# Quantised cross-attention and expert layer: first query among the keys, values quantised by chunk and transposed by DMA

## Chip, cores and metric

The kernel runs on one core of a Trainium2 chip. The metric is the device time of one execution in microseconds (us). The kernel is written engine by engine: TensorE (PE), VectorE (DVE), ScalarE (ACT), GpSimd (POOL) and SyncE (SP, which only issues DMAs) each have an instruction stream of their own and meet at semaphores.

## What is computed

2048 tokens (`x`, 4 x 512 rows) and 2048 context rows, both of width 512. One layer of cross-attention with 16 heads of 32 columns, then a mixture of 32 experts (4 for each token) and a shared expert. Only the attention, and of it only its preparation, is touched here:

```python
q = (layernorm(x) @ Wq + bq) / sqrt(32)        # 2048 x 512, 16 heads of 32
k, v = split(ctx @ Wkv + bkv)                  # 2048 x 512 each
q = fq_sym(q, axis=-1)                         # 8-bit, a scale for each row and head
k = fq_sym(k, axis=-1)                         # likewise
v = fq_sym(v, axis=rows)                       # 8-bit, ONE scale for each column, over all 2048 rows
p = fq_unsigned(softmax(q @ k.T))              # 8-bit probabilities, 2048 x 2048 for each head
x = x + (p @ v) @ Wp + bp
x = x + experts(layernorm(x))
```

The scale of a column of `v` needs that column's largest value over all 2048 context rows, so no value can be rounded before the last context row has been projected.

## The kernel before

**Keys phase.** `keys(g)` runs for g = 0 to 3, each time over four tiles of 128 context rows (i = 4g + r). PE transposes a context tile into the bank `psT` (L1579), ACT copies it out (L1457), PE projects keys (L1589, L1592). DVE rounds them (L1504 to L1512: largest value, scale, reciprocal, 8-bit, back to f32) and, with ACT (L1477, L1479), splits them into three bf16 parts; SP transposes the parts into `kT` by DMA (L1377, a 128 x 2048 bf16 transpose). DVE also takes the statistics of one tile of `x` (L539) and POOL normalises it (L587 to L609); SP stores it to `xn_dram` (L1357). At the end of each g, PE projects the values, turned, in four chunks m of 128 columns (L1608, 8 matmul passes each), ACT adds the bias and writes `vT[:, m, ...]` (L1469, semaphore `v_ev`), and DVE takes the largest value of each chunk (L1525 for g = 0, L1528 later).

**The bridge.** After g = 3, in this order. PE makes the first query tile: `pe_query(pe, 0, ...)`, four transposes (L385), ACT's copy (L1484), a bias matmul (L395) and eight passes (L396) into `psP`. DVE joins the maxima of the values (L1532), makes scale and reciprocal (L1551, L1553), rounds the four chunks to 8 bits, `vT8` (L1558, 128 x 2048 each), and only then rounds the query tile (L545, L551, L555). POOL widens chunks 0 and 1 to bf16, `vTb` (L1433), ACT chunks 2 and 3 (L1487). PE then transposes `vTb` in 16 blocks (L1629) into the banks `psT` and `psO`, which ACT (L1490) and DVE (L1563) copy in turn into `v`. POOL spreads the query tile (L622) and multiplies the four chunks of `Wp` by the values' scales (L1439); SP transposes the query tile by DMA into `qT[0]` (L1390). All engines wait for the last block of `v` before they enter the attention.

**Attention.** `pairs(eng, step)` runs 256 units (16 query tiles x 16 heads), written out by hand for each engine. In unit n PE makes scores of 128 queries x 2048 keys in two halves (L446) into `psS[0]` and `psS[1]`; DVE copies each half to `S` with its running maximum (L565, L581); POOL makes the bias (L638); ACT does the exponential to 8 bits, `p8` (L526); SP transposes `p8` by DMA into `pT` (L708); POOL widens to `pb` (L649), three units behind; PE multiplies by `v` (L461), LAG = 7 units behind. `S`, `p8`, `pT` and `pb` have four slots each, so unit n waits for unit n - 4. In between, in the same streams, the next query tile is made (heads 2 to 10) and earlier tiles are finished. Of the memory used by the keys phase, most is used again by the attention.

**Experts.** They follow when all units are done, from about 840 us on, and aren't touched.

Of the kernel before, what the change touches and what calls it, by code (L numbers as in the profile page):

```python
# [21 lines left out]
def attention_and_experts(nc, x, ctx_in, wq, wkv, wp, biases, bv, router, ebias, moe_w, out):  # L22
# [33 lines left out]
    with ExitStack() as es:  # L56
# [8 lines left out]
        psO = psAV[1]  # L65
# [65 lines left out]
        vT8 = cut(DC * TK // 4, I8).rearrange("p (c t) -> p c t", c=DC)  # L131
        k8 = cut(D // 4, I8)
        ks = [cut(D) for _ in range(2)]
# [3 lines left out]
        wkv_start = at[0]  # L137
# [3 lines left out]
        at[0] = phase_start  # L141
        S = [cut(TK) for _ in range(NS)]
        p8 = [cut(TK // 4, U8) for _ in range(NS)]
        pT = [cut(TK // 4, U16) for _ in range(NS)]
        pb = [cut(TK // 2, BF16).rearrange("p (j b q) -> p j b q", b=2, q=P) for _ in range(NS)]
# [4 lines left out]
        assert at[0] >= wkv_start  # L150
        qT = [cut(H * P // 2, BF16).rearrange("p (h q) -> p h q", h=H) for _ in range(2)]
        xn2T = cut(D).rearrange("p (c t) -> p c t", c=DC)

# [73 lines left out]
        v_cp_dve = sem("v_cp_dve")  # L227
# [53 lines left out]
        v_cp = sem("v_cp")  # L281
# [4 lines left out]
        v_tr = sem("v_tr")  # L286
        v_whole = sem("v_whole")
        v_whole_act = sem("v_whole_act")
# [83 lines left out]

        def pe_query(pe, t, stage):
# [13 lines left out]
            else:  # L387
                c = stage - 1
                if c == 0:
                    pe.wait_ge(query_ev, t + 1)  # L390
                    if due(t):
                        pe.wait_ge(q8_ready, t)
                    if due(t - 3):
                        pe.wait_ge(logits_cp, t - 3)
                    nc.tensor.matmul(psP[:], ones3[:], bias3[:, 0:D], start=True, stop=False)  # L395
                last = nc.tensor.matmul(psP[:], xnT[:, c, :], wq_sb[:, c, :], start=False, stop=(c == DC - 1))  # L396
# [41 lines left out]
        def pe_step(pe, tt, l):  # L438
# [102 lines left out]
        def dve_scale(dve, t):  # L541
# [3 lines left out]
            nc.vector.tensor_reduce(amax, hv(psP[:]), AX.X, ALU.max, apply_absolute_value=True).then_inc(q_amax, 1)  # L545

        def dve_whole(dve, t, p):
# [7 lines left out]
            nc.vector.scalar_tensor_tensor(hv(q8), hv(psP[:]), QSCALE, bc(rc, HD), ALU.mult, ALU.mult).then_inc(q8_ready, 1)  # L555
# [69 lines left out]
        def pool_step(pool, tt, l):  # L625
            n, p, h = PAIR * tt + l, l // H, l % H
            t = 2 * tt + p
            if there(t):
# [6 lines left out]
                if due(n - NS + 1):  # L635
# [3 lines left out]
                                            nsq[p][:, h:h + 1], LN255, ALU.mult, ALU.add).then_inc(bias_ready, 1)  # L639
            if not isinstance(n, int) or 0 <= n - BEHIND < TT * H:  # L640
# [36 lines left out]
        def sp_step(sp, tt, l):  # L677
# [32 lines left out]
            if h == 15 and there(t - 1):  # L710
# [3 lines left out]
                sp.dma_start(rows(out, t - 1), x1).then_inc(x1_stored, 16)  # L714

# [609 lines left out]
        def _(sp):  # L1325
# [65 lines left out]
            for b in range(2):  # L1391
                sp.wait_ge(keys_moved[b], 16 * KT // 2)
            sp.wait_ge(v_cp, KT // 2)
            sp.wait_ge(v_cp_dve, KT // 2)
# [9 lines left out]
        def _(pool):  # L1404
# [16 lines left out]
            for r in range(4):  # L1421
                normal(r, r)
            with pool.Fori(1, GK) as g:
# [3 lines left out]
            for m in range(DC // 2):  # L1427
                pool.wait_ge(v8_ready, m + 1)
                apart(pool, m + 1)
                if m == 0:  # L1430
                    pool.wait_ge(v_mm, 4 * GK)
                    pool.wait_ge(k_mm, KT)
# [253 lines left out]
```

## Time and profile before

| what | us |
|---|---|
| three runs | 1496.22, 1499.61, 1509.61 |
| median | 1499.61 |
| profiled execution, its own time | 1504.55 |
| span in the trace of that execution | 1502.6 |
| keys phase: start to the last value chunk out of PE | 0 to 149.8 |
| bridge: from there to the first score copy on DVE | 149.8 to 174.3 |
| attention units | 174.3 to about 841 |

The profile is one execution. Times in its views are microseconds from the start of the span. A row of the timeline gives start, duration, engine, line, operation, tiles, count, and in brackets how long the engine had been idle and what ended that. "SPq" rows are the time SP took to issue a DMA, not the transfer. The chain of waits is the chain of work that ended last, followed back step by step. The row of a stretch gives each engine's busy time in it, the clock that was granted to TensorE (1.00 is full speed) and the busy share of the 16 DMA engines.

### The profile page before, as it was taken

The page shows a single profiled execution, that of the slowest core. Times are in us where ns is not written, and L with a number is a line of the kernel's source. Part 1 is how long each engine was busy: PE and PEld are TensorE (multiplying, and loading weights), DVE is VectorE, ACT ScalarE, POOL GpSimd, SP SyncE. Part 2 cuts the span into 40 slices and gives each one's busy share as a digit, 9 for nine tenths or more (in the row PEclk, how much of TensorE's full clock was granted, in tenths as well). Part 3 has the DMA queues.
Part 4 walks back from the last instruction along what each step waited for, and adds up shares of the span by engine and source line. Part 5 has one row for each costly group of instructions (what it writes and reads, how often), then busy time and mean ns, then how long its engine had stood idle before and what let it go on. Part 6 is the DMA issues. An engine that isn't in the chain of part 4 may idle for free.

```text
span 1502.6 us, 28760 instructions
## 1 busy us (share of the span) xinstructions
PE 1300.7 (87%) x7954; PEld 647.3 (43%) x7955; DVE 989.5 (66%) x1847; ACT 794.2 (53%) x1022; POOL 871.5 (58%) x883
## 2 busy tenths in 40 slices
PE   7999678887888888888887588799999899999998
PEld 3333234443444444444444344344444444444443
DVE  7555699999999999999999257433333233323333
ACT  2222499998999999999999431122222121212221
POOL 3111388889899999999999403434343443444441
PEclk9999699999999999999999689999999999999999
DMA  9664178776676776676777365465666666665432
GB/s 267 159 157 98 32 130 142 135 141 133 140 146 142 141 144 133 139 141 139 145 137 131 103 247 183 158 180 112 190 186 188 190 151 162 158 179 123 83 57 72
DMA packets 387509, 217.60 MB, mean 145 GB/s; under 512 B 348279, under 2 KB 348407, under 8 KB 383234
## 3 DMA queue, kind: packets, MB, share of 16 engines
q1 hardware_dynamic: 369586, 182.34, 50.0%
q0 software_dynamic: 17872, 34.64, 12.5%
q8 instruction: 25, 0.41, 0.1%
q14 instruction: 26, 0.21, 0.1%
HBM read 104.47 MB, written 37.49 MB: 94 GB/s over the span
## 4 chain that ended last, share of the span: by engine, by line
PE 29%; issue 21%; DMA 17%; DVE 14%; POOL 10%; ACT 5%; SPq 2%; DVEq 2%; POOLq 1%; ACTq 0%
PE psS L773 14%; DMA out_y<-mem 11%; POOL mem L649 6%; DVE mem L565 4%; DVE mem L581 4%; PE psS L781 4%; DMA mem<-mem 3%; ACT mem L526 2%; PE psS L1608 2%; PE psS L446 2%; DMA mem<-xn_dram,mem 2%; POOL mem L638 1%; DVEq L1192 1%; PE psP L765 1%; PE psP L1589 1%
## 5 line engine op out<-in xcount | busy, mean ns | idle before, releaser
L526 ACT ACTIVATE mem<-mem 128x2048 uint8<-128x2048 f32 x256 | 535.3, 2093 | 46.0 <-POOL mem L638 41.2
L649 POOL TENSOR_SCALAR mem<-mem 128x2048 bf16<-128x2048 uint8 x256 | 486.2, 1899 | 28.3 <-DMA mem<-mem 9.2
L446 PE MATMUL psS<-mem 128*128 128x512 bf16 x1024 | 312.6, 388 | 97.8 <-DVE mem L565 49.1
L773 PE MATMUL psS<-mem 128*128 (+1 forms) x752 | 356.9, 617 | 0.1
L581 DVE TENSOR_SCALAR_CACHE_REDUCE mem<-psS,mem 128x1024 f32<-128x1024 f32 x256 | 328.1, 1282 | 0.9 <-PE psS L446 0.9
L565 DVE TENSOR_SCALAR_CACHE_REDUCE mem<-psS 128x1024 f32<-128x1024 f32 x256 | 313.0, 1223 | 15.0 <-PE psS L446 11.4
L807 DVE TENSOR_SCALAR mem<-psS 128x512 f32<-128x512 f32 x94 | 65.2, 693 | 344.3 <-PE psS L773 341.3
L1170 POOL DMA_INDIRECT out_y<-mem x78 | 124.0, 1589 | 189.3 <-DMA out_y<-mem 153.0
L801 ACT ACTIVATE mem<-mem 128x256 f32<-128x256 f32 x94 | 39.4, 419 | 360.8 <-DVE mem L807 360.8
L773 PEld LDWEIGHTS psS<-mem 128*128 128x128 f32 x752 | 139.9, 196 | 151.7 <-issue 148.8
L781 PE MATMUL psS<-mem 128*128 (+1 forms) x376 | 177.1, 592 | 1.0 <-ACT mem L795 1.0
L461 PEld LDWEIGHTS psAV<-mem 128*128 128x128 bf16 x4096 | 137.4, 96 | 86.9 <-POOL mem L649 36.7
L446 PEld LDWEIGHTS psS<-mem 128*128 128x128 bf16 x1024 | 67.9, 98 | 238.2 <-DVE mem L565 153.5
L1148 POOL DMA_INDIRECT mem<-xn_dram,mem x83 | 86.6, 1043 | 130.6 <-DVE mem L1281 91.1
L461 PE MATMUL psAV<-mem 128*128 128x32 bf16 x4096 | 142.7, 177 | 19.4 <-POOL mem L649 19.3
L789 ACT ACTIVATE mem<-psT 128x512 f32<-128x512 f32 x91 | 54.6, 600 | 123.7 <-PE psT L1201 90.7
L781 PEld LDWEIGHTS psS<-mem 128*128 128x128 f32 x376 | 70.9, 189 | 91.1 <-issue 89.7
L638 POOL TENSOR_SCALAR mem<-mem 128x1 f32<-128x1 f32 x256 | 68.0, 266 | 47.1 <-DVE mem L581 22.7
L1608 PE MATMUL psS<-mem 128*128 128x512 f32 x128 | 58.8, 613 | 9.5 <-ACT mem L1469 9.5
L396 PE MATMUL psP<-mem 128*128 128x512 f32 x128 | 66.5, 605 | 0.0
L1201 PEld LDWEIGHTS psT<-ident,mem 128*128 128x128 f32 x316 | 39.1, 142 | 63.4 <-issue 56.1
L417 PE MATMUL psAV<-mem 128*128 128x512 f32 x128 | 66.2, 602 | 0.0
(213 smaller groups left out, 1192.8 us busy)
## 6 DMA issues: line engine op xcount, KB each, us to landing
mem<-in_moe_w SPq DMA_DIRECT2D x33, 1536.0 KB, 8.1
xn_dram<-mem SPq DMA_DIRECT2D x33, 256.0 KB, 2.4
mem<-in_x SPq DMA_DIRECT2D x32, 256.0 KB, 3.1
mem<-xn_dram SPq DMA_DIRECT2D x32, 256.0 KB, 3.0
out_y<-mem SPq DMA_DIRECT2D x32, 256.0 KB, 2.3
mem<-mem SPq DMA_TRANSPOSE x288, 3.1
mem<-in_ctx_in SPq DMA_DIRECT2D x16, 256.0 KB, 3.2
mem<-out_y SPq DMA_DIRECT2D x16, 256.0 KB, 4.1
```

Of the source, the lines that this page charges most:

```text
L446: last = nc.tensor.matmul(psS[c][:, k * D:(k + 1) * D], qT[pm][:, hm, :], kT[:, hm, c * HALF + k * D:c * HALF + (k + 1) * D], start=True, ...
L461: last = nc.tensor.matmul(bank[:, ho * HD:(ho + 1) * HD], pb[slot][:, b // 2, b % 2, :], v[:, b, ho * HD:(ho + 1) * HD], start=(b == 0), s ...
L526: nc.scalar.activation(p8[slot], S[slot], ACT.Exp, bias=NB[:, slot:slot + 1], scale=sq[p][:, h:h + 1], accum_out=Z[p][:, h:h + 1]).then_in ...
L565: nc.vector.tensor_scalar(S[slot][:, 0:HALF], psS[0][:], 1.0, None, ALU.mult, ALU.max, accum_out=M[:, 2 * slot:2 * slot + 1]).then_inc(hal ...
L581: nc.vector.tensor_scalar(S[before][:, HALF:TK], psS[1][:], 1.0, M[:, 2 * before:2 * before + 1], ALU.mult, ALU.max, accum_out=M[:, 2 * be ...
L638: nc.gpsimd.tensor_scalar(NB[:, slot:slot + 1], M[:, 2 * slot + 1:2 * slot + 2], nsq[p][:, h:h + 1], LN255, ALU.mult, ALU.add).then_inc(bi ...
L649: nc.gpsimd.tensor_scalar(pb[slot], pT[slot].bitcast(U8).rearrange("p (j q b) -> p j b q", b=2, q=P), 1.0, 0.0, ALU.mult, ALU.add).then_in ...
L773: last = nc.tensor.matmul(bankG[o], xT[o if xo is None else xo][:, c, :], w(c * 2 * I, 2 * I), start=(c == 0), stop=(c == DC - 1))
L781: last = nc.tensor.matmul(bankY[o], hT[o][:, c, :], w(DC * 2 * I + c * D, D), start=(c == 0), stop=(c == I // P - 1))
L1148: nc.gpsimd.indirect_dma_start(out=xg[l], out_offset=None, in_=xn2_dram, in_offset=bass.IndirectOffsetOnAxis(list_column, 0), bounds_check ...
L1170: nc.gpsimd.indirect_dma_start(out=out, out_offset=bass.IndirectOffsetOnAxis(tile_rows[l][:, 0:1], 0), in_=y[l], in_offset=None, compute_o ...
L1608: last = nc.tensor.matmul(psS[m % 2][:, 0:D], wkv_sb[:, c, D + m * P:D + (m + 1) * P], cT[:, c, :], start=(c == 0), stop=(c == DC - 1))
```

## The change

1. The first query tile is made between `keys(0)` and `keys(1)`, on PE, ACT, DVE and POOL. It goes into `psS[1][:, D:2D]` in place of `psP`. Its DMA transpose into `qT[0]` (now in the memory of `ks`) is issued by SP after the last key transpose, ahead of the last store of normalised `x`.
2. On DVE the last group, `keys(3)`, is written out, and each value chunk is handled at once by `values(m)`: maximum, join, scale, reciprocal, rounding; then the next chunk.
3. POOL widens chunks 0 and 2, ACT chunks 1 and 3, with even and odd context rows put apart. SP transposes each by DMA straight into `v` (semaphore `v_moved`). PE's 16 blocks of transposes and the copies by ACT and DVE are gone.
4. No engine waits for `v` before the attention. PE waits for `v_moved` and `wp_scaled` in unit 7, POOL for `v_moved` ahead of the first `pb`. POOL scales `Wp` in units 0 and 1, two chunks in each. `pb` and `S` come first in the reused memory (`pb` lies over `vTb`), and `p8`, `pT`, `xn2T`, `qT[1]` lie behind `qT[0]`.

```diff
+        qT0 = mem[:, at[0]:at[0] + H * P // 2].bitcast(BF16).rearrange("p (h q) -> p h q", h=H)
+        ks = [cut(D) for _ in range(2)]
+        behind_keys = at[0]
...
+        def query_bank(t):
+            return psS[1][:, D:2 * D] if isinstance(t, int) and t == 0 else psP[:]
...
@@ pe_step @@
+                if isinstance(n, int) and n == LAG:
+                    pe.wait_ge(v_moved, 16 * DC)
+                    pe.wait_ge(wp_scaled, DC)
@@ pool_step, behind the bias of unit n, and ahead of pb @@
+                if isinstance(n, int) and n < DC // 2:
+                    for c in (2 * n, 2 * n + 1):
+                        nc.gpsimd.tensor_scalar(wp_sb[:, c, :], wp_sb[:, c, :], sv[:, c:c + 1], 1.0, ALU.mult,
+                                                    ALU.mult).then_inc(wp_scaled, 1)
...
+                if isinstance(m, int) and m == 0:
+                    pool.wait_ge(v_moved, 16 * DC)
@@ SP @@
             keys(GK - 1, False)
+            sp.wait_ge(q_spread, 1)
+            sp.dma_start_transpose(qT[0], qst.rearrange("p h j d -> p (h j d)")).then_inc(queries_moved[0], 16)
             store_normal(TT - 1, 3)
+            sp.wait_ge(query_tr, 1)
             sp.wait_ge(xn_stored, 16 * TT)
-            sp.wait_ge(query_tr, 1)
             sp.dma_start(xn, rows(xn_dram, 1)).then_inc(xn_in, 16)
-            sp.wait_ge(q_spread, 1)
-            sp.wait_ge(v_mm, 4 * GK)
-            sp.wait_ge(k_mm, KT)
-            sp.dma_start_transpose(qT[0], qst.rearrange("p h j d -> p (h j d)")).then_inc(queries_moved[0], 16)
...
+            for m in range(DC):
+                sp.wait_ge((v_whole, v_whole_act)[m % 2], m // 2 + 1)
+                sp.dma_start_transpose(v[:, :, m * P:(m + 1) * P], vTb[:, m, :]).then_inc(v_moved, 16)
             pairs(sp, sp_step)
@@ POOL @@
             for r in range(4):
                 normal(r, r)
+            pool.wait_ge(spread_zero, 1)
+            pool_scale(pool, 0, 0)
+            pool_spread(pool, 0)
...
+            for m in range(0, DC, 2):
                 pool.wait_ge(v8_ready, m + 1)
+                if m == 2:
                     pool.wait_ge(v_mm, 4 * GK)
+                nc.gpsimd.tensor_scalar(by_parity(vTb[:, m, :]), keyed(vT8[:, m, :]),
+                                            1.0, 0.0, ALU.mult, ALU.add).then_inc(v_whole, 1)
@@ ACT @@
             keys(0)
+            act.wait_ge(query_tr, 1)
+            nc.scalar.activation(xnT.rearrange("p c t -> p (c t)"), psT[:], ACT.Copy).then_inc(query_ev, 1)
             with act.Fori(1, GK) as g:
                 keys(g)
...
+            for m in range(1, DC, 2):
                 act.wait_ge(v8_ready, m + 1)
+                nc.scalar.activation(by_parity(vTb[:, m, :]), keyed(vT8[:, m, :]), ACT.Copy).then_inc(v_whole_act, 1)
@@ DVE, in keys(g) and behind it @@
+                    if last:
+                        values(m)
...
+            def values(m):
+                col = slice(m, m + 1)
+                dve.wait_ge(v_amax, KT + m - DC + 1)
+                nc.vector.tensor_tensor(svm[:, col], svm[:, col], vmax[:, col], ALU.max).then_inc(v_top, 1)
+                dve.wait_ge(v_top, GK - 2 + m + 1)
+                nc.vector.tensor_scalar(sv[:, col], svm[:, col], 1.0 / 127.0, 1e-8, ALU.mult, ALU.max).then_inc(v_scale, 1)
+                dve.wait_ge(v_scale, m + 1)
+                nc.vector.reciprocal(rv[:, col], sv[:, col]).then_inc(v_recip, 1)
+                dve.wait_ge(v_recip, m + 1)
+                if m == DC - 1:
+                    dve.wait_ge(xn_stored, 16 * TT)
+                nc.vector.tensor_scalar(vT8[:, m, :], vT[:, m, :], rv[:, col], None, ALU.mult).then_inc(v8_ready, 1)
...
             keys(0)
-            with dve.Fori(1, GK) as g:
-                keys(g)
+            dve_scale(dve, 0)
+            dve_whole(dve, 0, 0)
+            with dve.Fori(1, GK - 1) as g:
+                keys(g)
+            keys(GK - 1)
             pairs(dve, dve_step)
@@ PE @@
             keys(0)
+            pe.wait_ge(c_ev, 4)
             pe_query(pe, 0, 0)
             pe.wait_ge(w_q, 16)
             pe.wait_ge(bias_moved, 96)
             for stage in range(1, DC + 1):
                 pe_query(pe, 0, stage)
-            for b in range(KT):
-                if b >= 2:
-                    pe.wait_ge((v_cp, v_cp_dve)[b % 2], b // 2)
-                for m in range(DC):
...
+            with pe.Fori(1, GK) as g:
+                keys(g)
+            pe.wait_ge(c_ev, KT)
+            pe.wait_ge(k_whole, KT)
+            pe.wait_ge(v_ev, 4 * GK)
             for b in range(2):
                 pe.wait_ge(keys_moved[b], 16 * KT // 2)
             pairs(pe, pe_step)
```

## Rows read from the trace of the kernel before

**Rows 1.** The page: busy time, share of the span, instructions of each engine.

```profile
PE 1300.7 (87%) x7954; PEld 647.3 (43%) x7955; DVE 989.5 (66%) x1847; ACT 794.2 (53%) x1022; POOL 871.5 (58%) x883
```

**Rows 2.** Stretches: length, PE, PEld, DVE, ACT, POOL busy, clock, DMA share, GB/s.

```profile
150.00:187.50 37.50, 23.65 (x106) 11.28 (x105) 25.78 (x38) 16.06 (x18) 11.73 (x14) 0.68 0.15 31
225.00:300.00 75.00, 63.00 (x656) 33.12 (x655) 73.81 (x127) 68.63 (x72) 65.00 (x68) 1.00 0.81 139
```

**Rows 3.** The page, costliest groups: busy, mean ns, idle before and its releaser.

```profile
L649 POOL TENSOR_SCALAR mem<-mem 128x2048 bf16<-128x2048 uint8 x256 | 486.2, 1899 | 28.3 <-DMA mem<-mem 9.2
...
L581 DVE TENSOR_SCALAR_CACHE_REDUCE mem<-psS,mem 128x1024 f32<-128x1024 f32 x256 | 328.1, 1282 | 0.9 <-PE psS L446 0.9
L565 DVE TENSOR_SCALAR_CACHE_REDUCE mem<-psS 128x1024 f32<-128x1024 f32 x256 | 313.0, 1223 | 15.0 <-PE psS L446 11.4
```

**Rows 4.** Chain of waits across two group ends: start, us, what.

```profile
36.05 7.15 PE psS L1608 x16
...
48.89 0.70 DVE mem L1504
...
84.30 0.70 DVE mem L1504
```

**Rows 5.** Timeline: the first query tile on PE, and its load for it.

```profile
39.11 0.58 SPq L1379 DMA_DIRECT2D mem<-xn_dram  x1
...
149.65 0.60 PE L385 MATMUL psT<-ident,mem 128*128 128x128 f32 x4
...
151.56 3.70 PE L396 MATMUL psP<-mem 128*128 128x512 f32 x8
```

**Rows 6.** The line L1379 (that load): issue to landing.

```profile
DMA to landing us min/median/max: 3.0/3.0/3.0
```

**Rows 7.** Timeline of the last value chunks and the bridge.

```profile
142.78 1.28 DVE L1528 TENSOR_REDUCE mem<-mem 128x1 f32 x2
...
144.62 1.20 SPq L1357 DMA_DIRECT2D xn_dram<-mem  x1
...
146.50 0.69 ACT L1469 ACTIVATE mem<-psS,mem 128x512 f32 x1 [3.30 <-PE psS L1608]
...
149.94 0.69 ACT L1469 ACTIVATE mem<-psS,mem 128x512 f32 x1 [2.74 <-PE psS L1608]
...
150.76 0.69 DVE L1528 TENSOR_REDUCE mem<-mem 128x1 f32 x1 [2.75 <-ACT mem L1469]
...
152.28 8.15 DVE L1558 TENSOR_SCALAR mem<-mem 128x2048 int8<-128x2048 f32 x4
...
153.66 5.69 POOL L1433 TENSOR_SCALAR mem<-mem 128x2048 bf16<-128x2048 int8 x2 [9.61 <-DVE mem L1558]
...
160.46 1.91 ACT L1487 ACTIVATE mem<-mem 128x2048 bf16<-128x2048 int8 x1 [0.92 <-DVE mem L1558]
...
174.30 1.23 DVE L565 TENSOR_SCALAR_CACHE_REDUCE mem<-psS 128x1024 f32<-128x1024 f32 x1 [1.26 <-PE psS L446]
```

**Rows 8.** The line L1558: one instruction, min/median/max ns.

```profile
L1558 DVE TENSOR_SCALAR mem<-mem x4: 1279/2096/2920, 152.3 to 157.5; 128x2048 int8<-128x2048 f32 x4
```

**Rows 9.** Timeline of the first units, and the query transpose before them.

```profile
164.06 1.92 SPq L1390 DMA_TRANSPOSE mem<-mem  x1
...
179.30 0.27 POOL L638 TENSOR_SCALAR mem<-mem 128x1 f32<-128x1 f32 x1 [12.58 <-DVE mem L581]
...
183.94 5.32 SPq L708 DMA_TRANSPOSE mem<-mem  x3
...
187.17 1.90 POOL L649 TENSOR_SCALAR mem<-mem 128x2048 bf16<-128x2048 uint8 x1
```

**Rows 10.** The line L1390 (query transpose): issue to landing.

```profile
DMA to landing us min/median/max: 6.0/6.0/6.0
```

**Rows 11.** Stretches of the first units (columns as in group 2).

```profile
173.00:182.00 9.00, 6.77 (x17) 2.26 (x18) 6.20 (x12) 0.83 (x2) 0.54 (x2) 0.50 0.00 0
182.00:185.00 3.00, 1.87 (x7) 0.26 (x5) 3.00 (x5) 3.00 (x3) 0.27 (x1) 0.92 0.00 0
```

More of the change, by code:

```diff
@@ L141, in attention_and_experts @@
         at[0] = phase_start
+        pb = [cut(TK // 2, BF16).rearrange("p (j b q) -> p j b q", b=2, q=P) for _ in range(NS)]
         S = [cut(TK) for _ in range(NS)]
-        p8 = [cut(TK // 4, U8) for _ in range(NS)]
-        pT = [cut(TK // 4, U16) for _ in range(NS)]
-        pb = [cut(TK // 2, BF16).rearrange("p (j b q) -> p j b q", b=2, q=P) for _ in range(NS)]
         an = cut(D)
@@ L149, in attention_and_experts @@
         xn2 = cut(D)
-        assert at[0] >= wkv_start
-        qT = [cut(H * P // 2, BF16).rearrange("p (h q) -> p h q", h=H) for _ in range(2)]
+        at[0] = behind_keys
+        p8 = [cut(TK // 4, U8) for _ in range(NS)]
+        pT = [cut(TK // 4, U16) for _ in range(NS)]
         xn2T = cut(D).rearrange("p (c t) -> p c t", c=DC)
+        qT = [qT0, cut(H * P // 2, BF16).rearrange("p (h q) -> p h q", h=H)]
         at[0] = 0
@@ L280, in attention_and_experts @@
         v_top = sem("v_top")
-        v_cp = sem("v_cp")
         v_ev = sem("v_ev")
@@ L285, in attention_and_experts @@
         v_scale = sem("v_scale")
-        v_tr = sem("v_tr")
         v_whole = sem("v_whole")
+        v_moved = sem("v_moved")
         v_whole_act = sem("v_whole_act")
@@ L394, in pe_query @@
                         pe.wait_ge(logits_cp, t - 3)
[L395 to L396 removed]
+                    nc.tensor.matmul(query_bank(t), ones3[:], bias3[:, 0:D], start=True, stop=False)
+                last = nc.tensor.matmul(query_bank(t), xnT[:, c, :], wq_sb[:, c, :], start=False, stop=(c == DC - 1))
                 if c == DC - 1:
@@ L1520, in keys @@
                 for m in range(DC):
+                    last = isinstance(g, int) and g == GK - 1
+                    first = isinstance(g, int) and g == 0
                     dve.wait_ge(v_ev, 4 * g + m + 1)
-                    src = vT[:, m, bass.ds(g * D, D)] if not isinstance(g, int) else vT[:, m, g * D:(g + 1) * D]
-                    if isinstance(g, int):
-                        nc.vector.tensor_reduce(svm[:, m:m + 1], src, AX.X, ALU.max, apply_absolute_value=True).then_inc(
-                            v_amax, 1)
-                    else:
-                        nc.vector.tensor_reduce(vmax[:, m:m + 1], src, AX.X, ALU.max, apply_absolute_value=True).then_inc(
-                            v_amax, 1)
@@ L1530, in keys @@
-                dve.wait_ge(v_amax, 4 * g + DC)
-                if not isinstance(g, int):
-                    nc.vector.tensor_tensor(svm, svm, vmax, ALU.max).then_inc(v_top, 1)
-                    dve.wait_ge(v_top, g)
+                    part = vT[:, m, bass.ds(g * D, D)] if not isinstance(g, int) else vT[:, m, g * D:(g + 1) * D]
+                    nc.vector.tensor_reduce((svm if first else vmax)[:, m:m + 1], part, AX.X, ALU.max,
+                                                apply_absolute_value=True).then_inc(v_amax, 1)
@@ new lines, in keys @@
+                    if last:
+                        values(m)
+                if not last:
+                    dve.wait_ge(v_amax, 4 * g + DC)
+                    if not first:
+                        nc.vector.tensor_tensor(svm, svm, vmax, ALU.max).then_inc(v_top, 1)
+                        dve.wait_ge(v_top, g)
+            def values(m):
[10 more added lines that the diff above has]
+                nc.vector.tensor_scalar(vT8[:, m, :], vT[:, m, :], rv[:, col], None, ALU.mult).then_inc(v8_ready, 1)
@@ L1611, in _ @@
             keys(0)
-            with pe.Fori(1, GK) as g:
-                keys(g)
-            pe.wait_ge(c_ev, KT)
-            pe.wait_ge(k_whole, KT)
+            pe.wait_ge(c_ev, 4)
             pe_query(pe, 0, 0)
```

62 lines of the change are left out of this document (9 added, 53 removed).

## The prediction

> **What bounds the kernel now.** I read the busy shares first. TensorE leads with 87% of the span and VectorE has 66% [rows 1], but an average over four stages doesn't say what a change in one of them is worth. So next I cut the span into stretches. In 225 to 300 us, inside the attention, DVE is busy 73.81 of 75 us, and PE 63.00 [rows 2]. The groups say the same for all 256 units: DVE's two copies take 1223 and 1282 ns, 2.51 us a unit, and DVE stood idle before them only 15.0 and 0.9 us in all [rows 3]. The attention is one queue on DVE: the moment at which DVE takes up unit 0 sets the moment at which the attention ends, and the experts follow behind it.
>
> The stretch 150 to 187.5 is the hole: DVE 25.78 of 37.5 us, PE 23.65, DMA share 0.15 [rows 2]. The timeline there shows why. The last value chunk leaves ACT at 149.94 + 0.69 = 150.63. DVE finishes its maximum, rounds four chunks from 152.28 to 160.43, ACT's last widening ends at 162.37, sixteen blocks of PE transposes follow, and DVE takes up unit 0 at 174.30 [rows 7]. This is 23.7 us behind the last value chunk, and all of it is on the path.
>
> The keys phase, the third thing to read, is a ring and not one engine's queue: values on PE to 43.20, then context transposes and projections, and DVE's first key work of group 1 at 48.89; the same work of group 2 comes at 84.30, one period of 35.4 us later [rows 4]. PE can't run ahead, since its last two value chunks wait for ACT, which waits for DVE's key work. What is put on PE at the end of a group delays the whole ring.
>
> **Part 1, the query tile between groups 0 and 1: a cost.** PE does in the new place what it did after group 3: its transposes start at 149.65, the last pass ends at 151.56 + 3.70 = 155.26 [rows 5]. That is 5.61 us, ACT's copy included, and the transposes of the next context tile stand behind it on PE, with the projection of the keys and all of DVE's work waiting for them. I take +5.6. Could it be less? ACT and DVE are idle there, so their share is free: DVE's maximum, reciprocal and rounding (each at most the 0.70 of L1504, [rows 4]) and two small scales on POOL in between need some 2.8 us from the end of the query, while DVE isn't needed until 5.6 us after its 48.89, when the keys come. If all were hidden it would be 0; the ring above speaks against that. Could it be more? The load of the normalised tile is issued at 39.11 and lands 3.0 us later, at 42.1 [rows 5, 6]; PE wants it at 43.2, so it has 1.1 us in hand, and a wait of 1 us is my upper bound: 5.6 to 6.6. The query's removal from the bridge gives nothing back by itself: it lay behind DVE's rounding, which runs to 160.43.
>
> **Part 2, values by chunk.** I lay this on the times of before, and add 5.6 at the end. The DVE chain of one chunk is: maximum started at 150.76, rounding started at 152.28, thus 1.52 us, then the rounding [rows 7]. The rounding took 1279 ns at the least and 2920 at the most [rows 8]; the first, with POOL idle, is the short one, and POOL's widening runs across the others. POOL's L1433 took 2.85 us for one (5.69 for two) against 1.90 for the same count of elements in L649 [rows 3, 7], so the two engines slow each other. Chunk 0: its maximum starts at 142.78 as before, rounding 144.3 to 145.6. Chunk 1 (value already there): maximum from 145.6, rounding from 147.1, POOL widening chunk 0 from 145.7 to 147.6 (1.90) or later: to 148.7 at the least, if the rounding ends 1.1 us behind POOL as the last one did (160.43 against 159.35). Chunk 2 came from ACT at 147.19, no wait: POOL idle, 148.7 + 1.5 + 1.3 = 151.5. Chunk 3 came at 150.63: maximum from 151.5, rounding from 153.0 with POOL in chunk 2 from 151.6 to 153.5: to 154.6. That is the low end. The high end gives each of the two contested chunks 2.3 instead of about 1.6 and another 0.4 of waits: 156.4. I take the middle, 155.5.
>
> The rows show both engines stretched, 2.85 for 1.90 and 2.92 for 1.28 [rows 3, 7, 8]. The Trainium skill (SBUF — State Buffer, section "Who interferes with whom") says that DVE and GpSimd share a port pair which the first to start holds for its whole instruction, and that a DVE instruction with two SBUF inputs is blocked by a GpSimd instruction that reads SBUF. By that rule the join of the maxima, which has two inputs in memory, would also stand behind POOL in chunks 1 and 3, and chunk 3 would end at 156.4, the high end above, instead of 154.6; the forecast would be 0.9 us later.
>
> Written out or looped, `keys(3)` has the same instructions; I cost this at nothing.
>
> **Part 3, values by DMA: removed and hidden.** From 162.4 to 173.0 nothing else than PE, ACT and DVE moving blocks of `v` kept DVE from unit 0; this goes. What comes instead is on SP and the DMA engines. Before: SP's last store was issued at 144.62 [rows 7]. Now the query transpose takes that slot, 1.92 us to issue and 6.0 to land [rows 9, 10]: it lands at 150.6, when PE has its last `v_ev` (150.63): no wait, and PE has 4 us until DVE is free. The store follows at 146.5; were it to land as late as a transpose it would be 152.5, and DVE wants it for chunk 3 at 153.0: hidden with 0.5 in hand. The value transposes have the shape of the query's. SP issues chunk 0 at about 151.4, chunk 1 at 153.3, chunk 2 at 155.2; chunk 3 waits for ACT (155.5 + 1.9 = 157.4), so it lands at 157.5 + 6.0 = 163.5. Who waits? In the trace the first `pb` starts at 187.17, 12.9 us behind DVE's unit 0 [rows 7, 9]; now that is 155.5 + 12.9 = 168.4. Slack 4.9 us. If transposes can't overlap at all (6.0 each from 151.4), the last lands at 175.4, 7.0 late: the bound for a rival. SP's first `p8` transpose, 9.6 us behind unit 0 [rows 9], is at 165.1 and finds SP free at 159.4.
>
> **Part 4, units at once.** POOL's four multiplications of `Wp` go behind the biases of units 0 and 1. POOL is idle there: the bias of unit 0 comes 5.0 us behind DVE's start, and POOL had stood idle 12.58 us ahead of it [rows 9]; a multiplication has a quarter of the elements of L649's 1.90, about 0.5 us; two of them, even at 1.0 each, fit into the 2.2 us to the next bias. Cost 0. PE's new waits in unit 7 ask for what is long there. That `p8`, `pT` and `pb` lie elsewhere in memory costs nothing that I can name.
>
> **The sum.** Unit 0 on DVE: 155.5 + 5.6 = 161.1 against 174.3: 13.2 us saved, between 11.3 (156.4 + 6.6) and 14.1 (154.6 + 5.6). The profiled execution took 1504.55 (span 1502.6 and 1.95 around it): 1491.3. It lies 4.9 above the median of the three, 1499.61, so on the median: 1499.6 - 13.2 = **1486.4 us**. Own range of this case 1485.5 to 1488.3, and a few us for the medians (the three runs span 13.4 us).
>
> **Rivals.**
> - *The query's insertion is hidden* (the ring absorbs it): 18.8 us saved, 1480.8. For it: ACT, POOL and DVE are nearly idle from 43 to 48.9. Against it: PE isn't, and the rest waits for PE. It would also hold if group 1 had DMA waits that are now over earlier.
> - *The value transposes come late.* POOL's wait for `v_moved` stands ahead of the first `pb`, and the bias of unit 4 stands behind it; ACT's exponential and then DVE in unit 8 wait for it. 7.0 us late, less about 2 that the four slots absorb: 5 us lost, 1491.4. Against it: 4.9 us of slack. It decides at 163.5 + 4.9 = 168.4.
> - *TensorE's clock, the slow one.* From 173 to 182 the granted clock was 0.50, the lower level (1.2 GHz), and it was back (0.92) in 182 to 185 [rows 11]; before it fell, PE had nothing to do from 155.3 to 162.4. Now PE idles about 5 us between its first score and DVE's unit 0, and then has half-empty units. In the full units PE needs 63.00 of 75 us at full clock [rows 2]; at half clock 126, so each us spent at the low clock with full units costs 0.68. If the low clock lasts 19 us into the full units, the saving is gone (1499.6); at 41 us the kernel is over 1% slower, 1515. Against it: before, the clock was back before the first product with `v` began.
> - *Nothing gained*: another wait holds DVE at unit 0, for instance the key transposes. The store that SP issues behind them went out at 144.62 [rows 7], and with the 6.0 of the query's transpose they land by 150.6; nothing speaks for it.
>
> **How the numbers follow.** Chances: forecast 0.70, query hidden 0.08, transposes late 0.11, clock 0.07 (of it 0.04 beyond 1% slower), nothing gained 0.04. About 1% is what a measurement of this kernel can tell from no change, 15.0 us: 1484.6 and 1514.6. The forecast lies 1.8 us inside; of its 0.70 I give 0.25 to a measured gain of over 1% because the medians scatter by more than that. Faster 0.25 + 0.08 = 0.33; slower 0.04; the same 0.63. The range goes from the hidden query less a little, 1480, to the late transposes with scatter, 1496; beyond it lie nothing gained, most of the clock's case and the edges, under 0.2.
>
> **What would show it.** Group 1's first key work on DVE (48.89 before) at 54.5; the period of 35.4 unchanged; unit 0's L565 at about 161, right behind the last rounding with no wait for PE; the value transposes landing by 170; POOL's first `pb` behind a `p8` transpose and not behind `v`; DVE still at 2.5 us a unit. The prediction is wrong if the shift at 48.89 isn't 5.6, if DVE waits before unit 0, if DVE has gaps near unit 8, or if the clock stays at 0.5 past unit 7.

## The result and the profile after

| | before | after |
|---|---|---|
| median, first comparison (4 runs each) | 1503.37 | 1486.27 |
| range of these runs | 1496.22 to 1509.61 | 1484.62 to 1488.15 |
| profiled execution, span | 1502.6 | 1482.4 |
| unit 0 on DVE | 174.30 | 161.24 |
| last unit on DVE | 827.9 | 814.4 |

The ratio is 0.9894 (95% interval 0.9852 to 0.9937). A second comparison, with six runs of the changed kernel against eleven of the one before, gave 0.9903 (0.9874 to 0.9932). The change is worth about 1% of the time, 14 to 16 us. Both intervals lie clear of 1, but a gain of this size is no more than the 1% that the prediction took as the least that can be told from no change.

The page and one stretch of the attention, against [rows 1 to 3]. The stretch is moved by the 13 us with which unit 0 comes earlier:

```profile
PE 1284.7 (87%) x7890; PEld 635.9 (43%) x7891; DVE 988.0 (67%) x1848; ACT 787.8 (53%) x1014; POOL 869.5 (59%) x883
...
L585 DVE TENSOR_SCALAR_CACHE_REDUCE mem<-psS,mem 128x1024 f32<-128x1024 f32 x256 | 327.5, 1279 | 0.8 <-PE psS L447 0.7
L569 DVE TENSOR_SCALAR_CACHE_REDUCE mem<-psS 128x1024 f32<-128x1024 f32 x256 | 312.5, 1221 | 13.5 <-PE psS L447 9.0
```

```profile
212.00:287.00 75.00, 63.06 (x652) 32.54 (x650) 73.78 (x127) 68.17 (x71) 64.76 (x67) 1.00 0.75 138
```

The units cost DVE what they cost before (73.78 of 75 us, 1221 and 1279 ns); nothing in the attention became faster or slower. PE has 64 instructions fewer, the sixteen blocks of four transposes.

The bridge in the changed kernel, from its timeline (the columns are those of [rows 7]; these rows answer to them):

```profile
148.75 7.13 PE L1616 MATMUL psS<-mem 128*128 128x512 f32 x16 [1.94 <-ACT mem L1479]
...
150.06 1.29 DVE L1552 TENSOR_SCALAR mem<-mem 128x2048 int8<-128x2048 f32 x1
150.68 3.62 SPq L1400 DMA_TRANSPOSE mem<-mem  x1
151.26 0.68 DVE L1531 TENSOR_REDUCE mem<-mem 128x1 f32<-128x512 f32 x1
151.51 1.90 POOL L1448 TENSOR_SCALAR mem<-mem 128x2048 bf16<-128x2048 int8 x1 [1.39 <-DVE mem L1552]
151.98 1.44 DVE L1544 TENSOR_TENSOR mem<-mem 128x1 f32<-128x1 f32 x1
...
155.76 0.16 DVE L1544 TENSOR_TENSOR mem<-mem 128x1 f32<-128x1 f32 x1
...
157.11 10.20 SPq L1407 DMA_TRANSPOSE mem<-mem  x4
...
158.25 1.36 DVE L1544 TENSOR_TENSOR mem<-mem 128x1 f32<-128x1 f32 x1
...
160.04 1.29 DVE L1552 TENSOR_SCALAR mem<-mem 128x2048 int8<-128x2048 f32 x1
161.24 1.22 DVE L569 TENSOR_SCALAR_CACHE_REDUCE mem<-psS 128x1024 f32<-128x1024 f32 x1
```

Three things are to be seen. DVE goes from the last rounding (160.04) straight into unit 0 (161.24), with no wait for PE, SP or `v`. The four value transposes are issued behind its back. And the smallest instruction of the stretch, the join of two maxima of one element for each partition, took 1.44 and 1.36 us in chunks 1 and 3 where it took 0.16 in chunk 2: these are the two chunks in which POOL widens at the same time.

The new place of the query, same view, against [rows 4, 5]. The first row is the second pair of value chunks of group 0, sixteen passes on PE:

```profile
35.60 7.13 PE L1616 MATMUL psS<-mem 128*128 128x512 f32 x16 [2.30 <-ACT mem L1479]
...
42.57 0.60 PE L386 MATMUL psT<-ident,mem 128*128 128x128 f32 x4
...
44.39 3.70 PE L397 MATMUL psS<-mem 128*128 128x512 f32 x8
47.93 0.60 PE L1587 MATMUL psT<-ident,mem 128*128 128x128 f32 x4
48.20 0.69 DVE L549 TENSOR_REDUCE mem<-psS 128x16 f32<-128x512 f32 x1 [4.02 <-PE psS L397]
```

The next context transposes (L1587) stand behind the query, and DVE, which has been idle for 4.02 us, gets the query first and its keys only at 53.66.

**Where the time came from.** In what follows I read four marks in each trace. V0 is the start of the second pair of value chunks of group 0 on PE (36.05 before, 35.60 after). V3 is the same in group 3 (142.67 before, 148.75 after). Then come unit 0 and the last unit on DVE. From V3 to unit 0 the kernel before needs 31.63 us and the changed one 12.49, a gain of 19.14. V3 itself is 6.08 later. Unit 0 is therefore 13.06 earlier, and the last unit 13.5. The two spans differ by 20.2 us. Of the 6.7 that are left, 6.2 lie in the experts, counted from the start of the first of their matmuls (L773 before, L789 after) to the start of the last: 625.9 us before, 619.7 after. The experiments say what that is worth.

### The profile page after: what moved, and what is told of

The parts are those of the page before. It is cut to its first block, busy times and chain, and to the rows that moved or that the text cites. A ratio compares the mean times of both kernels' runs of the same rounds, so it can differ in the third digit from the quotient of the medians.

```text
span 1482.4 us, 28607 instructions
## 1 busy us (share of the span) xinstructions
PE 1284.7 (87%) x7890; PEld 635.9 (43%) x7891; DVE 988.0 (67%) x1848; ACT 787.8 (53%) x1014; POOL 869.5 (59%) x883
## 4 chain that ended last, share of the span: by engine, by line
PE 26%; issue 23%; DMA 19%; DVE 15%; POOL 10%; ACT 4%; POOLq 1%; SPq 1%; DVEq 1%; ACTq 0%
DMA out_y<-mem 16%; PE psS L789 12%; POOL mem L659 6%; DVE mem L569 4%; DVE mem L585 4%; PE psS L797 4%; ACT mem L530 2%; PE psS L447 2%; PE psS L1616 2%; POOL mem L642 2%; DMA mem<-mem 2%; PE psP L1597 1%; PE psP L781 1%; DMA mem<-xn_dram 1%; PE psAV L418 1%
## 5 line engine op out<-in xcount | busy, mean ns | idle before, releaser
L789 PE MATMUL psS<-mem 128*128 (+1 forms) x752 | 351.0, 609 | 0.1
L585 DVE TENSOR_SCALAR_CACHE_REDUCE mem<-psS,mem 128x1024 f32<-128x1024 f32 x256 | 327.5, 1279 | 0.8 <-PE psS L447 0.7
L569 DVE TENSOR_SCALAR_CACHE_REDUCE mem<-psS 128x1024 f32<-128x1024 f32 x256 | 312.5, 1221 | 13.5 <-PE psS L447 9.0
L789 PEld LDWEIGHTS psS<-mem 128*128 128x128 f32 x752 | 137.5, 193 | 147.8 <-issue 145.6
L797 PE MATMUL psS<-mem 128*128 (+1 forms) x376 | 177.1, 592 | 0.9 <-ACT mem L811 0.9
L642 POOL TENSOR_SCALAR mem<-mem 128x1 f32<-128x1 f32 x256 | 68.5, 267 | 36.1 <-DVE mem L585 12.5
L1217 PE MATMUL psT<-ident,mem 128*128 128x128 f32 x316 | 48.3, 276 | 21.6 <-DMA mem<-xn_dram,mem 21.6
```

Of the source, the lines that this page charges most:

```text
L569: nc.vector.tensor_scalar(S[slot][:, 0:HALF], psS[0][:], 1.0, None, ALU.mult, ALU.max, accum_out=M[:, 2 * slot:2 * slot + 1]).then_inc(hal ...
L585: nc.vector.tensor_scalar(S[before][:, HALF:TK], psS[1][:], 1.0, M[:, 2 * before:2 * before + 1], ALU.mult, ALU.max, accum_out=M[:, 2 * be ...
L642: nc.gpsimd.tensor_scalar(NB[:, slot:slot + 1], M[:, 2 * slot + 1:2 * slot + 2], nsq[p][:, h:h + 1], LN255, ALU.mult, ALU.add).then_inc(bi ...
L789: last = nc.tensor.matmul(bankG[o], xT[o if xo is None else xo][:, c, :], w(c * 2 * I, 2 * I), start=(c == 0), stop=(c == DC - 1))
L797: last = nc.tensor.matmul(bankY[o], hT[o][:, c, :], w(DC * 2 * I + c * D, D), start=(c == 0), stop=(c == I // P - 1))
```

## Experiments

One table for all, with the marks from each profiled execution. "Key gap" is from V0 to DVE's first key work of group 1; a star marks a V0 pair that was itself slow by 1.6 to 1.7 us, 8.7 to 8.8 instead of 7.13 (more on these slow pairs in the last section). "Attention" is from unit 0 to the last unit, "experts" from their first matmul to their last.

| kernel | key gap | V3 | unit 0 | V3 to unit 0 | attention | experts | ratio to before (95%) |
|---|---|---|---|---|---|---|---|
| before | 12.84 | 142.67 | 174.3 | 31.6 | 653.6 | 625.9 | 1 |
| after | 18.06 | 148.75 | 161.2 | 12.5 | 653.2 | 619.7 | 0.9894 (0.9852 to 0.9937) |
| r0_after_again | 19.66* | 147.19 | 159.7 | 12.5 | 653.0 | 615.4 | 0.9903 (0.9874 to 0.9932) |
| e1_query_first | 19.69* | 149.73 | 181.5 | 31.8 | 654.9 | 616.2 | 1.0041 (1.0010 to 1.0072) |
| e2_values_in_block | 18.06 | 149.65 | 165.5 | 15.9 | 653.5 | 625.2 | 0.9928 (0.9896 to 0.9959) |
| e3_values_by_pe | 18.06 | 149.06 | 175.5 | 26.5 | 655.2 | 613.0 | 0.9992 (0.9961 to 1.0022) |
| e4_values_late | 18.06 | 149.57 | 162.1 | 12.5 | 659.0 | 623.4 | 0.9920 (0.9891 to 0.9948) |
| e5_join_one_input | 18.06 | 150.13 | 161.5 | 11.3 | 654.7 | 633.3 | one run, not compared |
| e6_act_widens | 19.61* | 149.69 | 160.1 | 10.4 | 654.5 | 623.8 | 0.9904 (0.9873 to 0.9935) |
| e7_query_in_gaps | 12.91 | 140.71 | 153.4 | 12.7 | 654.4 | 622.4 | 0.9871 (0.9837 to 0.9904) |
| e9_gaps_again | 14.61* | 144.03 | 156.7 | 12.7 | 654.3 | 628.0 | 0.9872 (0.9833 to 0.9911) |
| e8_both | 12.91 | 141.47 | 151.9 | 10.4 | 651.9 | 623.0 | 0.9889 (0.9856 to 0.9923) |
| e10_both_again | 14.47* | 143.04 | 153.4 | 10.4 | 652.1 | 627.3 | 0.9868 (0.9834 to 0.9902) |

**The changed kernel again.**

> The changed kernel itself, once more and in more rounds. By the trace it saves 13.1 us at unit 0 and 13.5 at the last unit. If that is all, the ratio is 0.991 (13.5 of 1500); if something in the experts comes on top, as the 17 to 20 us of the first comparison suggest, the ratio is 0.987 to 0.989.

Ratio 0.9903, 14.5 us of 1500. In this trace unit 0 comes 14.6 us before that of the kernel before, in the first one 13.1. The experts' column settles the rest: their code is the same in all thirteen traces, and they take between 613.0 and 633.3 us from one execution to the next. The 6.2 us by which the first two traces differ there is of that kind. So it is not shown to be a gain of the change. It is also the likely reason why the kernel before ranged over 1491.56 to 1510.58 in the 31 runs beside e1 to e4, though those runs have no traces of their own.

**Part 1 alone,** in the kernel before; shown on PE, and the same on ACT, DVE and POOL.

```diff
+            pe.wait_ge(c_ev, 4)
+            pe_query(pe, 0, 0)
...
             with pe.Fori(1, GK) as g:
                 keys(g)
             pe.wait_ge(c_ev, KT)
             pe.wait_ge(k_whole, KT)
-            pe_query(pe, 0, 0)
```

> The kernel before with part 1 alone: the first query tile between groups 0 and 1; values, their PE transposes and the waits ahead of the attention as before. My theory (PE's ring delays all): DVE's first key work of group 1 comes 5.2 to 5.6 us later behind the values of group 0 on PE (12.8 us in the kernel before, about 18.1 here), nothing comes back in the bridge, unit 0 on DVE at 179.5 to 180, the kernel 5 us slower than before (ratio 1.003). Rival (the insertion is hidden): the interval stays at 12.8 or unit 0 at 174.3, ratio 1.000.

The key gap grew to 19.69, of which 1.6 is the slow V0 pair: 5.2 us for the query. V3 to unit 0 stayed at 31.8, so the bridge gave nothing back, and the kernel is 0.4% slower (1.0010 to 1.0072). The theory holds, and the rival, a hidden insertion, is out. Unit 0 came at 181.5 instead of 180; two slow value pairs instead of one make up the difference.

**Part 2 undone;** `values()` is now one join, scale and reciprocal over four columns and four roundings.

```diff
-                    if last:
-                        values(m)
...
+                else:
+                    values()
```

> The changed kernel with part 2 undone: all four maxima first, then one join, scale and reciprocal, then four roundings in a row; all else as changed. My theory (the early rounding is worth the overlap with PE's last two chunks): last maximum ends near 157.4, roundings from 158.2 to 166.4 with POOL's widening among them, unit 0 on DVE at 166.4 instead of 161.2, 5.2 us later. Rival (the port lock makes chunk-wise work as dear as block work): under 2.5 us later.

V3 to unit 0 is 15.9 instead of 12.5: 3.4 us, not the 5.2 I expected and not under 2.5. The four roundings took 6.51 us in a row here, where I had carried over the 8.15 of [rows 7]. With ACT on chunk 1, POOL's two widenings no longer stand one behind the other, and only the first of them holds up a rounding (the longest took 2.92 us, the others 1.27 to 1.29). The second starts 0.1 to 0.2 us behind the last rounding and does the waiting itself, 2.86 us instead of 1.90:

```profile
158.97 6.51 DVE L1552 TENSOR_SCALAR mem<-mem 128x2048 int8<-128x2048 f32 x4
...
160.42 2.79 POOL L1448 TENSOR_SCALAR mem<-mem 128x2048 bf16<-128x2048 int8 x1 [9.39 <-DVE mem L1552]
164.37 2.86 POOL L1448 TENSOR_SCALAR mem<-mem 128x2048 bf16<-128x2048 int8 x1 [1.17 <-DVE mem L1552]
```

**Part 3 undone.**

```diff
-            for m in range(DC):
-                sp.wait_ge((v_whole, v_whole_act)[m % 2], m // 2 + 1)
-                sp.dma_start_transpose(v[:, :, m * P:(m + 1) * P], vTb[:, m, :]).then_inc(v_moved, 16)
+            for b in range(KT):
+                if b >= 2:
+                    pe.wait_ge((v_cp, v_cp_dve)[b % 2], b // 2)
+                for m in range(DC):
+                    last = nc.tensor.transpose((psT, psAV[1])[b % 2][:, m * P // 2:(m + 1) * P // 2].bitcast(BF16),
+                                               vTb[:, m, b * P:(b + 1) * P], identb[:])
+                last.then_inc(v_tr, 1)
...
```

> The changed kernel with part 3 undone: v made by 16 blocks of PE transposes and copies of ACT and DVE, and all engines wait for the last one ahead of the attention. My theory: the last widening ends at 163.3, 16 blocks of 0.65 us follow, unit 0 on DVE at about 175, 13.5 to 14 us later than in the changed kernel; the whole kernel as slow as before or 1 us slower (the query's insertion stays and its gain is gone). Rival (the bridge's length came from the rounding, not the blocks): unit 0 by 167.

V3 to unit 0 is 26.5, 14.0 more than in the changed kernel, and the ratio 0.9992 (0.9961 to 1.0022). This edit also brings back the wait of every engine for `v` ahead of the attention, so it prices part 3 together with the waits of part 4: without both, no gain is left to be seen. Against e1, which has part 1 alone (31.8), V3 to unit 0 is 5.3 us shorter, and that is part 2 with the widenings in turn on POOL and ACT; it pays for the 5.2 us of the query in its new place. The net gain is that of parts 3 and 4.

**How much slack `v` has.**

```diff
+            for again in range(2):
+                sp.wait_ge(v_moved, 16 * (DC + again))
+                sp.dma_start_transpose(v[:, :, (DC - 1) * P:DC * P], vTb[:, DC - 1, :]).then_inc(v_moved, 16)
```

> The changed kernel with a later v: after the four value transposes SP waits for them and issues the last one twice more, one after the other, so v is complete some 9 us later (about 179 instead of 170) and SP takes up the first p8 transposes near 175.5 instead of 170.7. The output is unchanged. My theory (the first pb waits in POOL ahead of the bias of unit 4): first pb at about 180 instead of 175.3, DVE stands 2 to 4 us around unit 8, unit 0 unchanged, last unit 2 to 4 us later. Rival (the slots and the lag of seven units absorb it): DVE stands under 0.5 us more and the last unit comes as in the changed kernel.

The first `pb` came at 180.49, 18.4 us behind unit 0 where the changed kernel has 14.1 (175.30): 4.4 late. Unit 0 stayed where it is against V3, but the attention took 659.0 us instead of 653.2: 5.8 longer, and outside the 651.9 to 655.2 of all other traces. DVE stood 3.70 and 1.11 us, more than the 2 to 4 I expected, and the chain is another than the one I named. These are rows of the timeline, PE first:

```profile
178.17 0.59 PE L447 MATMUL psS<-mem 128*128 128x512 bf16 x2
182.53 0.58 PE L465 MATMUL psAV<-mem 128*128 128x32 bf16 x16 [3.76 <-POOL mem L659]
183.34 0.63 PE L447 MATMUL psS<-mem 128*128 128x512 bf16 x1 [0.22 <-issue]
```

```profile
180.49 1.90 POOL L659 TENSOR_SCALAR mem<-mem 128x2048 bf16<-128x2048 uint8 x1 [5.90 <-DMA mem<-mem]
...
184.01 1.28 DVE L585 TENSOR_SCALAR_CACHE_REDUCE mem<-psS,mem 128x1024 f32<-128x1024 f32 x1 [3.70 <-PE psS L447]
```

In step 7 PE's stream has the product of unit 0 ahead of the second half of scores of unit 6. PE waits there for `pb` 0, and DVE waits for the scores. PE's order decides, before POOL's bias of unit 4 does. In the changed kernel the first widening ended at 177.20 and PE's product started at 177.64, so the first `pb` has next to no slack: here 4.4 us of delay cost 5.8. `v` itself had some 5 us in the changed kernel: it landed by 170.0 (last issue 164.8, 5.2 at most to land). In e4 too it was not `v` that came last. Its last transpose was issued at 174.7 and landed by 179.2 (4.5 us at most), while the first `p8` transpose, which stands behind it in SP's stream, went out only at 176.46, and POOL started 4.0 us later. So e4 shows what a late first `pb` costs, through SP's queue; how late `v` alone may be was not run.

**What holds the join.**

```diff
-                nc.vector.tensor_tensor(svm[:, col], svm[:, col], vmax[:, col], ALU.max).then_inc(v_top, 1)
+                nc.vector.tensor_scalar(svm[:, col], svm[:, col], vmax[:, col], None, ALU.max).then_inc(v_top, 1)
```

> The changed kernel with the join of the maxima in values(m) made by a tensor_scalar: one input from memory and the other maximum as the scalar operand, in place of a tensor_tensor of two inputs; POOL still widens chunks 0 and 2. Theory A (what blocks the join is its second memory input): the joins of chunks 1 and 3 fall from 1.44 and 1.36 us to 0.2, and the rounding behind them now meets POOL's end and grows from 1.29 to about 2.0; unit 0 some 0.3 to 0.9 us earlier against the last value pair on PE (12.5 us). Theory B (any small DVE instruction is blocked while POOL widens): the joins stay at 1.4 us.

```profile
152.95 1.90 POOL L1448 TENSOR_SCALAR mem<-mem 128x2048 bf16<-128x2048 int8 x1 [1.45 <-DVE mem L1552]
```

```profile
153.42 0.21 DVE L1544 TENSOR_SCALAR mem<-mem 128x1 f32<-128x1 f32 x1
...
154.05 1.88 DVE L1552 TENSOR_SCALAR mem<-mem 128x2048 int8<-128x2048 f32 x1
```

The joins took 0.21 us, POOL widening all the while (152.95 to 154.85), and the roundings behind them 1.88 and 1.80 instead of 1.29. Theory A holds in both halves: what waits for POOL is the join as an instruction with two inputs, and the long rounding, not any small instruction. The edit changes the operation (tensor_tensor to tensor_scalar) together with the way the second value is read, so it doesn't part these two. Unit 0 gained 1.1 us against V3. The one run of the whole kernel took 1499.89 us, with the longest experts of all traces (633.3); it says nothing on the edit.

**All widenings on ACT,** chunk 0 in the last group, the others behind it.

```diff
                     nc.scalar.activation(dst, psS[m % 2][:, 0:D], ACT.Identity, bias=bvT[:, m:m + 1]).then_inc(v_ev, 1)
+                    if isinstance(g, int) and g == GK - 1 and m == 2:
+                        act.wait_ge(c_tr, KT)
+                        widen(0)
...
+            for m in range(1, DC):
+                widen(m)
```

> The changed kernel with all four widenings on ACT (chunk 0 between its copies of value chunks 2 and 3), none on POOL. Theory A (POOL's reads block the join of two inputs and the rounding on DVE, 1.3 us in each of chunks 1 and 3): no join over 0.2 us, every rounding 1.29, unit 0 on DVE 2.0 to 2.6 us earlier against the start of the last two value chunks on PE (12.5 us in the changed kernel). Theory B (the long joins come from something else, such as DMA traffic at that time): joins of 1.4 us stay and unit 0 doesn't move. Whole kernel: 0.998 of the changed one or less to be seen.

```profile
152.20 0.68 DVE L1530 TENSOR_REDUCE mem<-mem 128x1 f32<-128x512 f32 x1
152.91 0.16 DVE L1543 TENSOR_TENSOR mem<-mem 128x1 f32<-128x1 f32 x1
...
153.49 1.29 DVE L1551 TENSOR_SCALAR mem<-mem 128x2048 int8<-128x2048 f32 x1
```

```profile
157.44 5.50 ACT L1479 ACTIVATE mem<-mem 128x2048 bf16<-128x2048 int8 x3
...
166.92 2.08 ACT L530 ACTIVATE mem<-mem 128x2048 uint8<-128x2048 f32 x1
```

All joins took 0.16 us (chunk 1 is shown), all roundings 1.29, and V3 to unit 0 fell to 10.4, by 2.1: theory A again. ACT was done at 162.94, 4 us before its first exponential. The whole kernel (0.9904) shows none of it. Two microseconds are less than the half-width of this comparison's interval (0.0031, 4.7 us), so a gain in the whole time is not shown either way.

**The query in PE's idle times.** PE's `keys(g)`, now written out for all four groups:

```diff
+                if isinstance(g, int) and g == 1:
+                    pe_query(pe, 0, 0)
...
                 for m in range(DC):
+                    if isinstance(g, int) and g in (1, 2) and m == 2:
+                        pe_query(pe, 0, 2 * g - 1)
+                        pe_query(pe, 0, 2 * g)
```

> The changed kernel with the first query tile spread over PE's idle times: its transposes ahead of the values of group 1, its bias and two chunks behind the second value chunk of group 1, the other two at the same place of group 2, where PE waits some 2 us for ACT; DVE and POOL round and spread it behind group 2. Theory (the cost of part 1 is PE time in the wrong place, not PE time as such): the interval from the values of group 0 to DVE's first key work is back at 12.8 us instead of 18.1, groups 1 and 2 are longer by at most 0.5 us each, unit 0 about 4.5 us earlier than in the changed kernel, ratio to before 0.003 lower. Rival (any query work on PE lengthens the ring): unit 0 as in the changed kernel.

```profile
61.13 0.66 PE L386 MATMUL psT<-ident,mem 128*128 128x128 f32 x4
61.62 7.03 PE L1627 MATMUL psS<-mem 128*128 128x512 f32 x16
...
68.59 0.39 PE L396 MATMUL psS<-bias,ones 3*128 3x512 bf16 x1
68.90 1.98 PE L397 MATMUL psS<-mem 128*128 128x512 f32 x4
```

Half of the query's passes end at 70.88. ACT's copy of the first value chunk, for which the second pair waits, started at 70.19 and takes about 0.65, so the pair's start at 70.91 owes next to nothing to the query; the other half is in group 2. The key gap is back at 12.91, and unit 0 comes at 153.4, 7.8 us before the changed kernel's. Of this 5.2 is the query's PE time, which has gone into waits that PE had anyway (2.49 and 2.47 us ahead of the second pairs of groups 1 and 2 in the changed kernel). Another 3.35 are the slow value pairs of groups 1 and 2, two in the changed kernel's trace and none here (r0's trace has none there either, so this part isn't the same in every execution). Some 0.7 us go the other way, 0.2 of them behind V3. This trace has a slow pair as well, V3 itself (8.83), but it costs unit 0 only 0.2 (12.7 against 12.5 from V3): the last chunk's join, which then begins later, waits 0.67 us for POOL instead of 1.36. The ratio is 0.9871.

**Both together, and both kernels again.**

> All widenings on ACT and the query in PE's idle times together. Theory: the two gains add up, unit 0 some 6.5 us earlier than in the changed kernel, about 154.5, and the last unit as much; ratio to the kernel before 0.986 or 0.987 if the changed kernel's is 0.991. Rival (ACT becomes the last to be ready, its four widenings of 1.9 us stand behind its value copies): unit 0 on DVE early but its exponentials late, DVE standing in unit 4, and under 5 us earlier at the last unit.

> The kernel with the first query in PE's idle times once more, to part it from the changed kernel: 5.2 us less at unit 0 should give 0.9865 to 0.987 against the kernel before, where the changed kernel has 0.990. If the pairs of value chunks on PE of groups 1 and 2, now without the idle time ahead of them, again take 7.13 us and not 8.8, the slow pairs go with that idle time; if one of them is slow, they don't.

> The kernel with all widenings on ACT and the query in PE's idle times once more. By the trace unit 0 is 2.1 us earlier against the last value pair than in the kernel with the query alone; the ratio should be 0.985 to 0.987, up to 0.0014 below that kernel's. If it is again above it, the gain at unit 0 is given back later. The value pairs of groups 1 and 2 as for the other: 7.13 or 8.8 us.

In the trace the gains add up: key gap 12.91, V3 to unit 0 10.4, unit 0 at 151.9, 9.4 us before the changed kernel's, and ACT wasn't late. The medians of all runs are 1485.5 us for the changed kernel (10 runs), 1482.7 for the query in the gaps (12) and 1481.4 for both (12). Both variants lie below the changed kernel, but each of their intervals overlaps its interval, and 0.9889 and then 0.9868 for the same code shows how little a few runs part here. The best version is probably one of these two; that it beats the changed kernel by 3 to 4 us rests on the marks in the traces more than on the times.

## Why the prediction was right

The forecast was 1486.4 us, the measurement 1486.27. Unit 0 was forecast at 161.1 and came at 161.24. The agreement of the whole time to 0.1 us is luck: the forecast took 13.2 us from a median of 1499.61, but in the comparison the kernel before had 1503.37, so the medians differ by 17.1 (in the second comparison by 14.8). The mark at unit 0, 13.06 us earlier, is the fairer test. The terms under it were off in both directions, and the runs say by how much.

- **DVE's unit 0 sets the end: right.** Unit 0 came 13.06 us earlier, the last unit 13.5. In e4 it was the other way round: a stall inside the attention moved the last unit and left unit 0.
- **The query in its new place, 5.6 us: right in mechanism, 0.4 too dear.** The key gap grew by 5.22, and e1 alone shows it at the same price. The next context transposes started 5.36 behind the query's (42.57 to 47.93), not 5.61: the passes started 0.09 us sooner behind the transposes, since ACT's copy came sooner there, and the next transposes started 3.54 us behind the first pass, where I had counted its whole 3.70. The sign that I gave, a shift of 5.6 us at DVE's first key work of group 1, came as 4.77 (48.89 to 53.66), as V0 was 0.45 earlier in that trace.
- **Values by chunk, 12.8 us from V3 to unit 0: 12.5 measured,** by two errors that offset each other. I priced the chain of one chunk at 1.52 us from the four-column form of before; it took 1.30 (155.04 to 156.34). And I let chunks 1 and 3 wait only in their rounding. They waited in the join, 1.44 and 1.36, and then rounded in 1.29. The rule of the Trainium skill that I had set beside the sum (SBUF — State Buffer, section "Who interferes with whom") named this place, and by it I put unit 0 0.9 later; the place was right, as e5 and e6 show, and the surcharge was eaten up by the shorter chain.
- **Values by DMA off the path: right,** and with part 4 it is the whole net gain (e3). The transposes were dearer to issue, 2.55 us each instead of 1.92, and the query's took 3.62, against the 1.92 of [rows 9]. None of it reached DVE.
- **The slack of 4.9 us: right for `v`, and the wrong quantity.** I asked whether `v` comes before the first `pb`, and not whether the first `pb` comes before PE needs it. It came 14.1 us behind unit 0 instead of 12.9, because the first `p8` transpose took about 4.6 us from issue (170.71) to POOL's start, against 3.2 before [rows 9]; PE took it up 0.4 us after it was ready. The rival "late transposes" was priced through POOL's bias at 5 us for 7 us of delay; e4 lost 5.8 us for a first `pb` 4.4 late (4.8 of it are DVE's two waits). That case would have been dearer than I wrote.
- **Units at once: right.** POOL's two multiplications behind each of the two biases took 1.36 us in a stretch in which POOL was otherwise idle.
- **The clock.** In the first units it was as before: 0.50 in 162.5 to 165, and 1.00 in 168 to 173. The rival of a long slow clock didn't happen. But there was a term of the clock that I left out, in the keys phase. The changed kernel's trace has two slow value pairs where the one before has one, 1.65 us; the period from group 1 to group 2, which I had called unchanged at 35.4 us, was 36.73. My sum missed this, and the rest of the sum (the query 0.4, the chunks 0.3, an earlier first pair 0.45, and 0.3 that group 1 gave back) made up for it.

So the point is nearer to the measurement than its terms deserve: the mechanism was right, each term of unit 0 was within half a microsecond but for the slow pair, and the medians themselves scatter by more.

## What to carry to other kernels

Find the engine whose queue sets the end of the next stage, and ask what the moment is at which it can take that stage up; a whole bridge of other engines' work can then be moved behind that moment, as long as its consumer comes units later. When you move a step in time, look for the place where the engine waits anyway (e7), not merely for a place where the other engines are idle. And price slack at the last consumer in program order: here it was not POOL's wait for `v` but the first product in PE's stream, with 0.4 us in hand.

## What the runs showed of the hardware

- **A one-element instruction can be held for the length of another engine's.** The join, two inputs of one element for each partition, took 1.44 us and ended with POOL's widening of 1.90 (153.42 and 153.41); with one input and a scalar operand it took 0.21 (e5), and with the widenings on ACT 0.16 (e6). A shorter POOL instruction does it too: in e8 the join of chunk 0 began 0.40 us behind the start of POOL's L613 (0.76) and took 0.37, to POOL's end. In the changed kernel it began 0.12 us behind it and took 0.16, so a join that comes soon enough isn't held.
- **A slow pair of matmul chunks behind a short wait.** The sixteen passes of a value pair took about 7.1 us, or, when slow, 8.7 to 8.8. In the changed kernel, stretches around one of them (columns as in [rows 2]):

```profile
105.00:110.00 5.00, 5.00 (x12) 1.90 (x10) 3.63 (x9) 1.26 (x2) 1.79 (x4) 1.00 0.82 223
110.00:112.50 2.50, 0.05 (x1) 0.00 (x0) 1.90 (x4) 1.24 (x3) 0.75 (x2) 1.00 1.04 221
112.50:115.00 2.50, 2.48 (x4) 1.16 (x5) 1.40 (x3) 0.55 (x1) 1.03 (x2) 0.66 0.84 242
115.00:120.00 5.00, 5.00 (x11) 2.10 (x10) 0.69 (x1) 0.69 (x1) 0.00 (x0) 0.83 0.76 199
```

  PE had been fully busy to 110, then had 0.05 us of work in 2.5, and the granted clock was 0.66 in the next 2.5 and 0.83 in the 5 behind them, a part of each at the lower level (1.2 GHz). What was missing to full speed, 0.34 x 2.5 + 0.17 x 5 = 1.70 us, is what the pair lost (8.83 - 7.13). In groups 1 and 2, which have such a wait ahead of the second pair, 12 of 18 pairs were slow over nine traces (one of them 10.17); in the four traces in which the query fills these waits, 0 of 8. In the last group no pair was slow in those nine traces, where PE had waited 1.65 to 1.96 us, but both traces of the kernel with the query alone in the gaps had one (8.83 and 8.79), with an unfilled wait of 2.59 and 2.58. In group 0 PE waited 2.29 to 2.31 in all thirteen traces, and 5 of the 13 pairs were slow. So filling the wait takes the slow pair away at its place; what decides about it elsewhere stays open.
